# Six tiles' results parked in the join buffers, and the joins moved from ScalarE to SyncE, in a two-layer attention and expert kernel

## What is computed

```python
xn = _layernorm(x, axis=-1)
x = x + _L1_attn_ref(xn, ...) + _L1_ffn_ref(xn, ...)
...
logits = jnp.einsum('nc,ec->ne', xf, w_router)
probs = jax.nn.softmax(logits, axis=-1)
topw, topi = jax.lax.top_k(probs, TOP_K)
...
h = jax.nn.gelu(jnp.einsum('nc,ecd->ned', xf, w1) + b1[None, :, :], approximate=False)
expert_out = jnp.einsum('ned,edc->nec', h, w2) + b2[None, :, :]
out = jnp.einsum('ne,nec->nc', wdense, expert_out)
```

## Time and profile before

| what | value |
|---|---|
| median of 3 runs | 913.72 us (912.93 to 915.83) |
| profiled execution, its own time | 911.97 us |
| its span | 910.3 us |
| PE busy | 834.7 us (92%) |
| DVE busy | 700.4 us (77%) |
| POOL busy | 621.6 us (68%) |
| ACT busy | 576.1 us (63%) |
| chain that ended last | PE 59%, DVE 25%, issue 5%, ACT 5%, POOL 4%, DMA 2% |

### The profile page before, as it was taken

How to read it: one execution, slowest core, us unless ns; L and a number is a source line. 1 busy time by engine, 2 the same in 40 slices (tenths; PEclk the granted TensorE clock), 3 DMA queues, 4 the chain that set the end, 5 groups by cost and what they waited for, 6 DMA issues and landing times.

```text
span 910.3 us, 22670 instructions
## 1 busy us (share of the span) xinstructions
PE 834.7 (92%) x7975; PEld 744.4 (82%) x7975; DVE 700.4 (77%) x1809; ACT 576.1 (63%) x1183; POOL 621.6 (68%) x598
## 2 busy tenths in 40 slices
PE   3789999999899999998898989898899899999996
PEld 3678878989799999986665666666899899999996
DVE  7787777886576998897899998898664555667776
ACT  5766465444477667769887777573666566666661
POOL 4156676777304788777888888887777777666663
PEclk9999999999999999999999999999999999999999
DMA  9799997115649999962111111115664665588985
GB/s 268 234 373 357 361 353 258 50 50 161 244 143 270 311 314 279 277 212 75 40 43 37 39 40 44 37 44 187 220 186 151 199 193 189 165 246 273 285 276 174
DMA packets 131136, 174.30 MB, mean 191 GB/s; under 512 B 15825, under 2 KB 85969, under 8 KB 130769
## 3 DMA queue, kind: packets, MB, share of 16 engines
q1 hardware_dynamic: 96864, 124.43, 42.8%
q0 software_dynamic: 16640, 34.37, 11.5%
q10 hardware_dynamic: 17520, 14.06, 5.1%
HBM read 93.96 MB, written 80.97 MB: 192 GB/s over the span
## 4 chain that ended last, share of the span: by engine, by line
PE 59%; DVE 25%; issue 5%; ACT 5%; POOL 4%; DMA 2%; SPq 0%; DVEq 0%; ACTq 0%; POOLq 0%
PE pair L923 14%; PE pair L892 6%; PE pair L861 5%; PE pair L862 5%; PE pair L863 5%; PE pair L695 3%; PE pair L782 3%; DVE a_en L1622 3%; POOL sent L2064 2%; DVE X L1555 2%; PE pair L702 2%; DVE stats_t L1184 2%; PE pair L704 2%; PE pair L703 2%; DVE X L1642 1%
## 5 line engine op out<-in xcount | busy, mean ns | idle before, releaser
L2064 POOL DMA_INDIRECT sent<-a_rows,slot x224 | 220.9, 986 | 77.8 <-issue 57.4
L2075 POOL DMA_INDIRECT ex_joined<-outs,slot x128 | 136.4, 1066 | 82.5 <-DMA outs<-ex_tile_out 45.6
L2166 POOL DMA_INDIRECT back<-ex_tile_out,address x136 | 150.1, 1104 | 59.2 <-issue 31.4
L861 PE MATMUL pair<-ex_x_hi,ex_w_hi 128*128 128x256 f32 x497 | 146.9, 296 | 0.0
L862 PE MATMUL pair<-ex_x_lo,ex_w_hi 128*128 128x256 f32 x497 | 140.7, 283 | 0.0
L863 PE MATMUL pair<-ex_x_hi,ex_w_lo 128*128 128x256 f32 x497 | 140.5, 283 | 0.0
L923 PE MATMUL pair<-ex_down_all,ex_hid 128*128 x1136 | 133.3, 276 | 1.1 <-ACT ex_hid L1888 0.8
L923 PEld LDWEIGHTS pair<-ex_down_all,ex_hid 128*128 128x128 f32 x1136 | 129.7, 192 | 2.7 <-issue 2.7
L1762 ACT ACTIVATE ex_w_hi<-ex_stage 128x768 fp32r<-128x768 f32 (+1 forms) x72 | 67.5, 937 | 69.6 <-DMA ex_stage<-in_experts 69.6
L1888 ACT ACTIVATE ex_hid<-pair,ex_stage 128x256 f32<-128x256 f32 x284 | 107.7, 494 | 4.5 <-PE pair L863 2.2
L863 PEld LDWEIGHTS pair<-ex_x_hi,ex_w_lo 128*128 128x128 f32 x497 | 95.1, 191 | 0.0
(11 more groups left out here) (253 smaller groups left out, 2021.3 us busy)
## 6 DMA issues: line engine op xcount, KB each, us to landing
outs<-v_heads SPq DMA_DIRECT2D x8, 4352.0 KB, 37.3
ex_stage<-in_experts SPq DMA_DIRECT2D x72, 322.0 KB
ex_stage<-in_experts SPq DMA_DIRECT2D x72, 320.0 KB, 5.1
ex_tile_in<-sent SPq DMA_DIRECT2D x72, 128.0 KB
outs<-ex_tile_out SPq DMA_DIRECT2D x71, 128.0 KB
ex_joined<-back ACTq DMA_DIRECT2D x15, 512.0 KB, 5.9
ex_tile_in<-sent SPq DMA_DIRECT2D x54, 132.0 KB
X<-in_x SPq DMA_DIRECT2D x16, 256.0 KB, 5.3
```

The lines of the kernel that those rows point to most:

```text
L861: pe.matmul(o[:, of_half], wh, x_hi[i % 2][:, of_half], start=True, stop=False)
L2064: pool.indirect_dma_start(out=sent[layer], out_offset=bass.IndirectOffsetOnAxis(ap=slot_i[layer][k][:, s, j:j + 1], axis=0), in_=rows[laye ...
L2075: pool.indirect_dma_start(out=joined[g % NJOIN][:, j, k, :], out_offset=None, in_=outs, in_offset=bass.IndirectOffsetOnAxis(ap=slot_i[0][k ...
L2166: pool.indirect_dma_start(out=back, out_offset=bass.IndirectOffsetOnAxis(ap=address[i % NSIDE][:, s // HALF, s % HALF:s % HALF + 1], axis= ...
```

## The change

Its parts, all in the second layer:

- **Tiles.** `EARLY` is 7: the first 12 tiles hold rows of groups 0 to 7, and SyncE waits for all sends before tile 12.
- **Transfers of the attention steps.** Gathers run in steps 3 to 9 and sends in the steps that they leave; steps 5 to 15 have six to eight transfers each, steps 18 and 19 ten and nine. From step 16 (`LATE_STEP`) on none waits for PE. The whole quarter 3 is sent after the last step (`SENDS_LAST`), without waits.
- **Parked results.** The results of tiles 0 to 5 are written into the halves of the three join buffers (`home`, `results_of`), not into `tile_out`. POOL's give-backs begin with tile 6, and those of the parked tiles follow those of tiles 8 and 10 to 14 (`BACK_ORDER`).
- **Side values.** Every tile has addresses of its own (`address_of`, in the first layer's slots and four more), gates have two buffers, and DVE's waits for results ahead of both go, and for the first ten tiles those ahead of b2o.
- **Joins and additions.** SyncE issues the joins, behind the weights of tiles 28 to 35 (`JOINS`), in turns one and two; DVE adds in passes 26 to 34 (`ADDS`), ACT stores one pass after (`STORES`).

```diff
-         {2: ((0, 0, 8),), 3: ((0, 8, 16),), 4: ((0, 16, 20),), 5: ((0, 20, 24),), 10: ((0, 24, 32),),
-          11: ((1, 0, 8),), 12: ((1, 8, 16),), 13: ((1, 16, 24),), 14: ((1, 24, 32),),
-          15: ((2, 0, 8),), 16: ((2, 8, 16),), 17: ((2, 16, 24),), 18: ((2, 24, 32),), 19: ((3, 0, 8),), 20: ((3, 8, 16),)})
-SENDS_LAST = {0: (3, 16, 24), 1: (3, 24, 27), 2: (3, 27, 30), 3: (3, 30, 32)}
-EARLY = 6
+         {2: ((0, 0, 8),), 5: ((0, 8, 9),), 6: ((0, 9, 14),), 7: ((0, 14, 15),), 9: ((0, 15, 18),), 10: ((0, 18, 25),), 11: ((0, 25, 32),),
+          12: ((1, 0, 7),), 13: ((1, 7, 14),), 14: ((1, 14, 22),), 15: ((1, 22, 29),), 16: ((1, 29, 32), (2, 0, 5)),
+          17: ((2, 5, 13),), 18: ((2, 13, 23),), 19: ((2, 23, 32),)})
+SENDS_LAST = (3, 0, 32)
+EARLY = 7
...
+LATE_STEP = 16
...
-NSTAGE, NIN, NOUT, NJOIN, NSIDE, AHEAD = (8, 4), 4, 4, 3, 6, 6
+NSTAGE, NIN, NOUT, NJOIN, NGATE, AHEAD = (8, 4), 4, 4, 3, 2, 6
+
+
+NEXTRA = 2 * NJOIN
...
-GATHERS = {4: ((11, 0, 4),), 5: ((11, 4, 8),), **{n - 6: ((n, 0, 8),) for n in range(12, 16)}}
-
-LAST_JOIN = {max(2 * g + 9, 2 * EARLY + 9 + g): g for g in range(14)}
-LAST_ADD = {n + 2: g for n, g in LAST_JOIN.items() if g < 13}
-LAST_STORE = {n + 4: g for n, g in LAST_JOIN.items() if n + 4 < NTILES}
+GATHERS = {3: ((11, 0, 8),), 4: ((12, 0, 7),), 5: ((12, 7, 8), (13, 0, 6)), 6: ((13, 6, 8),), 7: ((14, 0, 6),),
+           8: ((14, 6, 8), (15, 0, 4)), 9: ((15, 4, 8),)}
+
+JOINS = {28: (0,), 29: (1, 2), 30: (3,), 31: (4, 5), 32: (6,), 33: (7, 8), 34: (9,), 35: (10, 11)}
+ADDS = {26: (0,), 27: (1, 2), 28: (3,), 29: (4, 5), 30: (6,), 31: (7, 8), 32: (9,), 33: (10, 11), 34: (12,)}
+STORES = {n + 1: groups for n, groups in ADDS.items() if n + 1 < NTILES}
...
+FIRST_BACK = {8: 0, 10: 1, 11: 2, 12: 3, 13: 4, 14: 5}
+BACK_ORDER = [m for n in range(NEXTRA, LAST_BACK + 1) for m in ((n, FIRST_BACK[n]) if n in FIRST_BACK else (n,))]
...
-        address = [sb(f"address{i}", [P, 2, HALF], I32) for i in range(NSIDE)]
+        gate_t = [sb(f"gate_t{i}", [P, 4, 2, HALF]) for i in range(NGATE)]
+        address_more = [sb(f"address{i}", [P, 2, HALF], I32) for i in range(NTILES - K * NS * ST // SUB)]
...
+        def home(i):
+
+            n = i - NTILES
+            return NOUT + n if 0 <= n < NEXTRA else i % NOUT
+
+        def results_of(i):
+
+            h = home(i) - NOUT
+            if h < 0:
+                return tile_out[home(i)][:]
+            return joined[h // 2][:].rearrange("p s k c -> p (s k) c")[:, SUB * (h % 2):SUB * (h % 2 + 1), :]
+
+        def address_of(n):
+
+            per = NS * ST // SUB
+            if n >= K * per:
+                return address_more[n - K * per][:]
+            return slot_i[0][n // per][:].rearrange("p s (t h j) -> p (s t) h j", h=2, j=HALF)[:, n % per, :, :]
+
         def results_dma(i):
-            return (put_dma, ret_dma)[i // NTILES][i % NOUT]
+            h = home(i) - NOUT
...
+                for g in JOINS.get(n, ()):
+                    results_back(sp, NTILES + last_tile(1, g))
+                    load_results(sp, NG + g)
+            for g in range(sum(map(len, JOINS.values())), NG):
+                results_back(sp, NTILES + min(last_tile(1, g), LAST_BACK))
+                load_results(sp, NG + g)
...
-                if n >= NSIDE:
-                    j = i - NSIDE
-                    dve.wait_ge(results_dma(j), returned(j))
...
-                dve.scalar_tensor_tensor(address[i % NSIDE][:], other, 0.0, r[:, :, :, TOK2], ALU.not_equal, ALU.add).then_inc(side_ready, 1)
+                dve.scalar_tensor_tensor(address_of(n), other, 0.0, r[:, :, :, TOK2], ALU.not_equal, ALU.add).then_inc(side_ready, 1)
...
-                dve.wait_ge(results_dma(i - NOUT), returned(i - NOUT))
+                gate = gate_t[i % NGATE][:, 3, :, :].rearrange("p h s -> p (h s)")
+                if n >= NEXTRA + NOUT:
...
-                if n in LAST_ADD and n <= LAST_BACK + 1:
-                    collect1(LAST_ADD[n])
+                for g in ADDS.get(n, ()):
+                    collect1(g)
...
-                if n in LAST_JOIN:
-                    results_back(act, NTILES + last_tile(1, LAST_JOIN[n]))
-                    load_results(act, NG + LAST_JOIN[n])
-                if n in LAST_STORE:
-                    store(LAST_STORE[n])
-
-            for g in range(len(LAST_STORE), NG):
-                if len(LAST_JOIN) <= g + 2 < NG - 1:
-                    results_back(act, NTILES + last_tile(1, g + 2))
-                    load_results(act, NG + g + 2)
+                for g in STORES.get(n, ()):
+                    store(g)
+
+            for g in range(sum(map(len, STORES.values())), NG):
...
-                    if s >= 1:
+                    if s >= 1 and n >= NEXTRA:
                         behind_tile1(n + 2, s - 1)
-                    pool.indirect_dma_start(out=back, out_offset=bass.IndirectOffsetOnAxis(ap=address[i % NSIDE][:, s // HALF, s % HALF:s % HALF + 1], axis=0),
-                                            in_=tile_out[i % NOUT][:, s, :], in_offset=None).then_inc(ret_dma[i % NOUT], 16)
+                    pool.indirect_dma_start(out=back, out_offset=bass.IndirectOffsetOnAxis(ap=address_of(n)[:, s // HALF, s % HALF:s % HALF + 1], axis=0),
...
-                        behind_attention1(g, e, y, i)
+                        if step < LATE_STEP:
+                            behind_attention1(g, e, y, i)
...
-                transfer(7)
-
-            for n in range(NTILES):
-                if n in SENDS_LAST:
-                    s, first, end = SENDS_LAST[n]
-                    for i, jk in enumerate(range(first, end)):
-                        if n == 0:
-                            behind_tile1(i // NC1, i % NC1)
-                        else:
-                            behind_tile1(n + 1 + (i + 3) // NC1, (i + 3) % NC1)
-                        send(1, s, jk)
-                if n <= LAST_BACK:
-                    give_back(n)
+                for i in range(7, len(gathers) + len(sends)):
+                    transfer(i)
+
+            s, first, end = SENDS_LAST
+            for jk in range(first, end):
+                send(1, s, jk)
+            for n in BACK_ORDER:
+                give_back(n)
```

More of the change, by code:

```diff
@@ L447, in build @@
         down_done, side_ready, out_ready = sem("down_done"), sem("side_ready"), sem("out_ready")
-        gathered_dma = [[sem(f"gathered_dma{i}{half}") for half in range(2)] for i in range(NJOIN)]
+        join_half_dma = [[sem(f"join_half_dma{i}{half}") for half in range(2)] for i in range(NJOIN)]
         joined_dma = [sem(f"joined_dma{i}") for i in range(NJOIN)]
@@ L936, in last_tokens @@
                         m = pe.matmul(bank[7][:, i * C:(i + 1) * C], is_of[:, SUB * (n - LAST_BACK - 1) + s, i * P:(i + 1) * P],
[L937 removed]
+                                      results_of(NTILES + n)[:, s, :], start=(first and s == 0 and i == 0),
                                       stop=(last and s == HALF * halves(n) - 1), skip_group_check=True)
@@ L1702, in vector_program @@
             weigh1(NTILES - 1)
-            for n, g in LAST_ADD.items():
-                if n > LAST_BACK + 1:
-                    collect1(g)
-            for g in range(len(LAST_ADD), NG - 1):
+            for g in range(sum(map(len, ADDS.values())), NG - 1):
                 collect1(g)
```

28 lines of the change are left out of this document (14 added, 14 removed).

## The result

The changed kernel took 963.63 us (median of 4 runs, 958.36 to 965.07) beside 914.78 us of the kernel before (median of 4, 912.93 to 917.65): a ratio of 1.0521 [1.0469, 1.0572], so **slower**. Predicted were 966 us, with a range of 938 to 1000. The profiled execution took 965.07 us (span 963.4).

The account below looks back on a forecast made before the run. PE bounds the expert stage, no single engine the attention steps. Tile 10 -5.2, attention steps -2, tail -1, joins +58.3, clock +2 sum to +52 us: 964 profiled, 966 as median, range 938 to 1000.

Parts of the forecast that it names:

- +3.0: DVE's passes with two joins: the second join lands 3.0 us after the first, between 1.8 by rate and 5.8.
- Clock: Expert stage's end: PE at 1.2 GHz is hidden in passes 26 to 33, the last two tiles pay +2 us.
- The gain at tile 10: PE's wait for rows before tile 10 goes: -5.2 us, covered by over 20 us of room at tile 12.
- now no give-back precedes the sends, so the last is made near 688: POOL after the last root: without 12 give-backs (15.3 us) the last send moves from 702.89 to near 688.
- Room of 8 us, so nothing waits: Tile 19's buffer: sixteenth give-back done at 782, weighing at 790, so no wait for give-backs.
- rival (4): Parked tiles make POOL late, so SyncE blocks at its first join: 11 us more, 977 us; chance 0.04.
- Few engines wait for them: Attention steps: POOL's masks and roots come 1.27 us earlier, gaining only -2 us, bounds +2 and -18.
- The tail: After the last tiles: group 12 added in pass 34, both last joins go out together, -1 us, bounds 0 and -2.
- the largest term: Joins in passes 26 to 33: DVE releases each join, then stands until it lands; 58.3 us later.
- (1): Joins queue fully behind the weights in SyncE's queue: +106 us, 1019 us; chance 0.10.
- (2): Joins land sooner because ACT's stores and SyncE's weights pause while DVE stands: +31 us, 944 us; chance 0.15.
- (3): Joins are hidden within DVE's slack and the gains stand: 905.5 us; chance 0.04.

Follow-up runs that it names:

- the old tables: Changed kernel with joins two tiles earlier, attention steps' tables of gathers and sends as before the change: 910.36 us, ratio 0.9923.
- the parked ones later: Changed kernel with joins two tiles earlier, parked tiles given back behind tiles 8, 11, 13, 15, 17, 19: 906.58 us, ratio 0.9887.
- the waits kept: Changed kernel with joins two tiles earlier, POOL's transfers of steps 16 to 19 waiting for PE as before: 906.7 us, ratio 0.9885.
- the root first: Changed kernel with joins two tiles earlier, six sends moved from step 18 to 19, behind the last root: 911.67 us, ratio 0.9949.

## Why the prediction was right, and where it was not

**Joins.** The mechanism and its size held. Issue at 1.4 us after the weighing: 1.39. Landing: 5.8 us chosen, median 5.9 (3.9 to 8.1) measured. Passes with one group, from one x_lo to the next, predicted at 12.8 us: 13.0, 12.7 and 13.1. Passes with two, predicted at 15.8: 14.6, 15.2, 15.8 and 14.0, a mean of 14.9. The term that was too large is the second join, "+3.0" for its landing behind the first. Its addition started 0.34 to 1.08 us after the end of the first, whose two halves take 1.4: so 1.7 to 2.5 us. The lower bound by the window's rate, 1.8, was nearer. PE's first wait was 4.78 us (5.0 predicted). PE's transposes of the 35th tile came 936.64 us after the start, 884.34 before, and with the 25th down product 2.45 us early that is 52.3 + 2.45 = 54.8 us for the joins, against 58.3.

The Trainium skill, "DMA: Bandwidth & Descriptors", section "Anatomy of one DMA — SWDGE (gpsimd) path", fits a transfer that GpSimd issues as 2.0 us and its bytes at 436 GB/s, which for a join gives an estimate of 3.2 us; the joins here are issued by SyncE. The least of the sixteen was 3.9, so here too the trace does not agree.

**Clock.** From those transposes to the down product behind them PE needed 942.09 - 936.64 = 5.45 us, at a clock of 0.52, and 887.38 - 884.34 = 3.04 before: 2.4 us, against 2 predicted. Inside the passes, PE's work at 1.2 GHz hid behind DVE's wait, as predicted, though only a part of it was at that level (0.81 granted on average over the stretch): DVE never waited for PE before the weighings of passes 27 to 33. 54.8 + 2.4 are the 57.2 of the table.

**The gain at tile 10.** The wait is gone, 5.2 us as predicted, and two experiments show that it takes both parts: with ten tiles and parked results it is back, with twelve tiles and none parked another takes its place. But the step "**now no give-back precedes the sends, so the last is made near 688**" failed. POOL's timeline of the kernel after, which answers to the earlier trace rows:

```profile
645.66 1.87 POOL L2088 DMA_INDIRECT sent<-a_rows,slot  x1 [0.30 <-issue]
647.55 1.04 POOL L2210 TENSOR_TENSOR rms<-rms,halves_of 128x4 f32<-128x4 f32 x1
...
704.82 0.96 POOL L2088 DMA_INDIRECT sent<-a_rows,slot  x1 [0.30 <-issue]
706.09 0.97 POOL L2190 DMA_INDIRECT back<-ex_tile_out,slot  x1 [0.30 <-issue]
```

The last send came at 704.82, 49.0 us after the first down product, 48.9 before. I counted the give-backs that leave this stretch and not the sends that enter it. Between the last root and the last send POOL made 32 sends and 12 give-backs before, and makes 41 sends now: all 32 of quarter 3, and nine of quarter 2 that step 19 leaves behind the root. So 44 transfers became 41, not 32, and the root itself stood 8.2 us ahead of the first down product, where it had stood 10.1 ahead. Tile 12's rows were asked for at 711.53 and were there without a wait, so it cost nothing; but the room was not the 20 us that the prediction names as its cover.

**"Room of 8 us, so nothing waits"** failed too. DVE waited 4.48, 4.91, 2.76, 0.69 and 0.99 us ahead of b2o for give-backs (13.8 us in all, the last of the waits shown above). The prediction has the give-backs start at 701, at 1.27 us a transfer, and the sixteenth, which frees tile 19's buffer, done at 782 for a weighing at 790. POOL's last transfer of that give-back, and DVE behind it:

```profile
792.60 0.96 POOL L2190 DMA_INDIRECT back<-ex_tile_out,slot  x1 [0.30 <-issue]
```

```profile
794.89 0.42 DVE L1555 TENSOR_TENSOR ex_b2o<-ex_stage,bo 128x256 f32<-128x256 f32 x1 [4.91 <-DMA back<-ex_tile_out,slot]
```

The first transfer went at 706.09, 5 us later than predicted. From there to 792.60 it is 86.5 us for 63 distances, 1.37 us each, since some transfers lasted 1.4 to 1.8 us where the prediction had 0.97 for all: 6 us more. The last one's landing, for which the sum had no term, adds the rest: 2.3 us passed from its issue to b2o. Together 13 us, and the room was 8. The late last send has little part in it: in the experiment with the old tables it came 15 us earlier, and DVE waited 4.25 and 6.02 us all the same. The order of the give-backs is what removed the waits, in the experiment with the parked ones later.

DVE's slack took nearly all of it; one down product came 7.53 us after the last, 0.7 late. That is most of the distance between -5.2 predicted and -4.2 measured up to the 25th tile. So POOL was late with the parked tiles between, as rival (4) has it, but not late enough to hold up SyncE's first join, which was issued 1.39 us after the weighing.

**The attention steps.** -2 us predicted, -5.4 measured: the term was too small, though the bounds of +2 and -18 held it. "Few engines wait for them" was not shown. The old tables took 4.4 us of it back (239.5 against 235.1), the waits kept 1.9 (237.0), the root first nothing (234.4); each is one profile. Why fewer transfers per step gain this much stays open.

**The tail.** -1 predicted, 17.9 to 16.3 us measured.

**Sum.** -5.4 - 4.2 + 54.8 + 2.4 - 1.6 = +46 us in the code that was changed, +52 predicted; 7.2 us more of the profile are the first layer's own variation. The kernel before went from 913.72 us in the times that were known to 914.78 in the runs beside the kernel after, and the medians differ by 48.9 us. That the forecast of 966 lies within 3 us of 963.63 is in part luck: the largest term was 3.5 us too high, the attention steps' gain 3.4 too small, and the kernel before came out 1.1 us above the time that the forecast started from. Without that, the sum was 6 us off, well inside the range.

**Rivals.** (1), a join passing fully behind the weights, is out: with 0.85 us of weights issued ahead, joins landed in 5.9. (2), the short landing beside paused transfers, is out as well: the DMA share over the stretch did fall from 0.95 to 0.59, but not while the joins were in flight (0.91 beside the first, last section), and the median landing was no shorter. (3) is what the change becomes with the joins two tiles earlier: 904.85 us measured where the prediction gave 905.5.

## What to carry to other kernels

Before an operation is moved, look for what releases it, and compare the place of the release with the place of the consumer on the in-order engine: if the release stands right ahead of the consumer, the whole trip (issue, landing, addition) becomes idle time in every pass, however early in the program both stand. A lead of one period was nearly enough where the trip (8.6 us) was little more than a period (6.87), a lead of two was safe in either queue. And count, for a queue such as POOL's, what enters a stretch as well as what leaves it: here 12 transfers left, nine came, and the last one stood where it had been. Two parts of a change may gain only together: the twelve tiles without parking met another wait, parking without them kept the old one.
